# Tree layer: leaf rows fetched by index and summed late, with the last sums inside the attention behind it

## The reference, cut to what matters

```python
def _L0_ffn_ref(oldx, W_in, b_in, W_out):     # x: 2048 tokens of 256
    logits = x @ W_in.T + b_in                # 2048 x (8 * 255)
    decisions = (logits > 0).astype(jnp.int32).reshape(B, PAR, N_NODES)
    acts = jax.nn.silu(logits).reshape(B, PAR, N_NODES)
    current = jnp.zeros((B, PAR), dtype=jnp.int32)
    dmap = jax.nn.one_hot(current, N_NODES, dtype=acts.dtype)
    for d in range(DEPTH):                    # DEPTH = 7
        ...                                   # follow the decision one level down
        dmap = dmap + jax.nn.one_hot(current, N_NODES, dtype=acts.dtype)
    masked = acts * jax.lax.stop_gradient(dmap)
    out = masked.reshape(B, WIDTH) @ W_out.T
```

## Time and profile before

| | |
|---|---|
| median of 3 runs | 1630.63 us (1630.32 to 1631.8) |
| profiled execution | 1630.92 us, span 1629.2 us |
| PE busy | 1438.7 us, 88% |
| DVE busy | 1072.1 us, 66% |
| ACT busy | 755.6 us, 46% |
| POOL busy | 116.5 us, 7% |
| mean granted clock | 0.953 |

### The profile page before, as it was taken

How to read it: one execution, slowest core, us unless ns; L and a number is a source line. 1 busy time by engine, 2 the same in 40 slices (tenths; PEclk the granted TensorE clock), 3 DMA queues, 4 the chain that set the end, 5 groups by cost and what they waited for, 6 DMA issues and landing times.

```text
span 1629.2 us, 26350 instructions
## 1 busy us (share of the span) xinstructions
PE 1438.7 (88%) x9842; PEld 1074.1 (66%) x9849; DVE 1072.1 (66%) x2358; ACT 755.6 (46%) x1264; POOL 116.5 (7%) x168
## 2 busy tenths in 40 slices
PE   7999999878897996799989999999988889999557
PEld 5666666557783443477786878787764677788446
DVE  4455575778877874687866465655458988886344
ACT  2211212257773666376672222222224877788323
POOL 1000000000000000111000000000010011001323
PEclk9999999989998997899998999999998999999779
DMA  9462202320000000000008910000100000010166
GB/s 323 167 207 78 78 1 78 127 85 14 14 3 0 1 1 1 25 14 1 14 2 265 303 43 1 1 1 0 33 7 7 1 7 2 7 31 24 41 186 180
DMA packets 60285, 96.62 MB, mean 59 GB/s; under 512 B 11091, under 2 KB 48972, under 8 KB 59982
## 3 DMA queue, kind: packets, MB, share of 16 engines
q1 hardware_dynamic: 57742, 78.50, 15.0%
q10 hardware_dynamic: 544, 12.16, 2.2%
q0 software_dynamic: 1872, 4.27, 0.7%
HBM read 73.21 MB, written 37.30 MB: 68 GB/s over the span
## 4 chain that ended last, share of the span: by engine, by line
PE 50%; issue 18%; DVE 15%; ACT 6%; DVEq 4%; DMA 2%; SPq 1%; POOL 1%; ACTq 1%; POOLq 1%
PE bank L1997 8%; PE bank L1998 8%; PE bank L1689 7%; PE bank L1667 7%; DVE MB L927 3%; PE bank L1794 3%; DVE plo L945 2%; PE bank L1845 2%; PE bank L1595 1%; PE bank L1765 1%; PE bank L1799 1%; PE bank L1798 1%; DMA jx<-copy_routed 1%; DVE raw L1211 1%; PE bank L1767 1%
## 5 line engine op out<-in xcount | busy, mean ns | idle before, releaser
L945 DVE TENSOR_TENSOR plo<-e,phi 120x512 f16<-120x512 f32 x256 | 179.1, 705 | 50.2 <-ACT phi L1419 46.5
L1413 ACT ACTIVATE e<-bank 120x512 f32<-120x512 f32 x256 | 150.6, 588 | 42.7 <-PE bank L1799 34.3
L927 DVE TENSOR_REDUCE MB<-bank 128x4 bf16<-128x480 f32 x256 | 155.9, 646 | 15.1 <-PE bank L1767 11.5
L1419 ACT ACTIVATE phi<-e 120x512 f16<-120x512 f32 x256 | 161.2, 630 | 8.8
L1344 ACT ACTIVATE act<-bank,bin 127x512 f32<-127x512 f32 x64 | 43.1, 687 | 167.2 <-DVE dec L757 163.2
L1667 PE MATMUL bank<-xT,winT 128*127 128x512 f32 (+1 forms) x256 | 114.6, 593 | 1.3 <-ACTq L1315 1.3
L1689 PE MATMUL bank<-woutT,msk 128*128 128x256 f32 (+1 forms) x512 | 115.1, 379 | 0.0
L676 DVE TENSOR_SCALAR high<-raw 128x512 int32<-128x512 int32 x96 | 41.0, 427 | 108.1 <-ACT raw L1548 60.9
L1689 PEld LDWEIGHTS bank<-woutT,msk 128*128 128x128 f32 (+1 forms) x512 | 96.8, 190 | 15.4
L556 POOL TENSOR_TENSOR veps<-mv,ceps 128x4 f32<-128x4 f32 x32 | 8.9, 278 | 1336.7 <-DVEq L647 1204.9
L1997 PE MATMUL bank<-hah,h1w 128*128 128x512 f32 x256 | 101.3, 396 | 3.6 <-DVE hal L679 3.6
(11 more groups left out here) (308 smaller groups left out, 3518.8 us busy)
## 6 DMA issues: line engine op xcount, KB each, us to landing
copy_routed<-zeros SPq DMA_DIRECT2D x1, 17028.0 KB
jw<-copy_experts SPq DMA_DIRECT2D x23, 385.0 KB, 3.3
seen<-in_h1T SPq DMA_DIRECT2D x8, 512.0 KB, 7.2
seen<-in_h2T SPq DMA_DIRECT2D x8, 512.0 KB, 4.9
h1w<-copy_h1T SPq DMA_DIRECT2D x1, 4096.0 KB, 16.7
h2w<-copy_h2T SPq DMA_DIRECT2D x1, 4096.0 KB, 14.3
ctxp<-in_ctxT SPq DMA_DIRECT2D x13, 240.0 KB, 3.0
jx<-copy_routed SPq DMA_DIRECT2D x23, 132.0 KB, 3.1
```

Source lines behind the costliest of these rows:

```text
L927: dve.tensor_reduce(MB[:, t, h0 // 8, SK + h0 % 8:SK + h0 % 8 + 4], b[:, 0:4 * SK].rearrange("p (h k) -> p h k", h=4), AX.X, ALU.max).then ...
L945: dve.tensor_tensor(plo[:, g % 3, :], e32[:, g % 3, :], phi[:, g % 3, :], ALU.subtract).then_inc(s.lo, 1)
L1413: act.activation(e32[:, g % 3, :], bank[2 + g % 3][0:SK, :], ACT.Exp).then_inc(s.exp, 1)
L1419: act.activation(phi[:, g % 3, :], e32[:, g % 3, :], ACT.Copy).then_inc(s.phi, 1)
```

## The change

The leaf part of the dense products is replaced. Of all four pairs, 32 steps (`STEPS`) are now counted through, and `tree_step(g)` on each engine says what it does in step g, for itself and for older steps:

- Layer 0's attention gets transposes of the leaf columns of `winT` on PE in its last two pairs and copies on ACT into `table`; ACT and SP write `leaves`, a table in HBM with, for each of 1024 leaves, its output row (256), its input row (256) and its bias: 2052 bytes. The 1 MB load of the leaves' `woutT` falls away.
- Only inner nodes are multiplied densely: half the logits, one silu, one mask, half the output products.
- From the count of the leaves ACT makes a one-hot `hot` (a Relu of 128x512, bf16), PE multiplies it with the leaf numbers (four products of one column), and DVE writes the row number `idx`.
- POOL gathers the rows: four indirect transfers of 128 rows for each step, into one of five buffers `rowsG`.
- Four steps behind, DVE takes the dot of each token's normalised row with its leaf's input row (`leaf_logits`, four instructions with a running sum), and ACT the silu (`leaf_values`, four of one column) and three scaled identity matrices `dgl`.
- Five steps behind, PE adds three of the four tiles (`turned_leaves`, identity matrix times rows, into the sums' banks) and DVE the fourth, straight to x (`add_leaves`).
- The sums of two pairs lie in different banks, and normalised rows in two buffers. A pair's residual follows in the sixth step of the next pair.
- `low_bits` is one OR of each slice into `seen_low`; the test for the low bits comes once, at the end. Slices are spread over the steps.
- The five weight copies are issued in steps 3, 9, 14, 19 and 24 instead of before the stage, and the first mask of L1X is loaded at the start.
- Steps 34 to 37 (the last dots, values and sums and the last residual) stand on PE, ACT and DVE behind the first four steps of L1X. L1X on PE waits for the last residual only before its first `values`, and DVE for the turned sums of step 27.

The core of the diff:

```diff
+STEPS, ROW, GB, LAG = PAIRS * TREES, 2 * D + 1, 5, 5
+SUMS = (4, 0)
+TURNED = (0, 1, 2)
...
+        def gather(g):
+            pool.wait_ge(Tf.row, g + 1)
+            if g >= GB:
+                pool.wait_ge(Tf.added, g - GB + 1)
+                pool.wait_ge(Tf.turned, g - GB + 1)
+            for t in range(TT):
+                pool.indirect_dma_start(rowsG[g % GB][:, t, 0:ROW], None, leaves[:],
+                                        bass.IndirectOffsetOnAxis(idx[:, g % TREES, t:t + 1], 0),
+                                        bounds_check=TREES * LEAVES - 1, oob_is_err=False).then_inc(landed[g % GB], 16)
...
         def low_bits(i, q):
-            dve.tensor_scalar(seen_low[:], seen[:, q, :].bitcast(I32), 0xFFF, None, ALU.bitwise_and)
-            dve.drain()
-            dve.tensor_reduce(lowmax[:, ds(i * SEEN + q, 1)], seen_low[:], AX.X, ALU.max)
+            dve.tensor_tensor(seen_low[:], seen_low[:], seen[:, q, :].bitcast(I32), ALU.bitwise_or)
...
+        def leaf_logits(g):
+            rows_in = (xln, xln_odd)[g // TREES % 2]
+            dve.wait_ge(landed[g % GB], got(g))
+            for t in range(TT):
+                if t == 2:
+                    dve.drain()
+                last = dve.scalar_tensor_tensor(out=dots[:, t % 2, :], in0=rows_in[:, t, :], scalar=1.0,
+                                                in1=rowsG[g % GB][:, t, D:2 * D], op0=ALU.mult, op1=ALU.mult,
+                                                accum_out=lv[:, g % GB, t:t + 1])
+            dve.drain().then_inc(Tf.dot, 1)
...
+            def tree_step(g):                          # DVE
+                i, p = g // TREES, g % TREES
+                if g < STEPS and (p or not i):
+                    decisions(g)
+                if 1 <= g <= STEPS:
+                    masked(g - 1)
+                if 4 <= g < STEPS + 4:
+                    leaf_logits(g - 4)
+                if g == 2 * TREES:
                     weight_scales()
+                if 1 <= g <= STEPS:
+                    leaf_numbers(g - 1)
+                if 5 <= g < STEPS + 5:
+                    add_leaves(g - 5)
+                if g < STEPS and not p and i:
+                    decisions(g)
+                if g >= TREES and g % TREES == LAG % TREES:
+                    tree_residual((g - LAG) // TREES - 1)
...
+        def hot_leaves(g):
+            act.wait_ge(Bf.cnt, g + 1)
+            if g >= 2:
+                act.wait_ge(Tf.idx, g - 1)
+            act.activation(hot[:, g % 2, :], bank[7][:, :], ACT.Relu, bias=onec[:, 0:1]).then_inc(Tf.hot, 1)
+
+        def leaf_values(g):
+            act.wait_ge(Tf.dot, g + 1)
+            if g >= 2:
+                act.wait_ge(Tf.turned, g - 1)
+            for t in range(TT):
+                last = act.activation(val[:, g % GB, t:t + 1], lv[:, g % GB, t:t + 1], ACT.Silu,
+                                      bias=rowsG[g % GB][:, t, 2 * D:ROW])
+            act.drain()
+            for n, t in enumerate(TURNED):
+                last = act.activation(dgl[:, g % 2, n, :], ident[:], ACT.Copy, scale=val[:, g % GB, t:t + 1])
+            last.then_inc(Tf.val, 1)
...
+            def tree_step(g):                          # PE
+                if g < STEPS and (p or not i):
+                    tree_logits(g)
+                if i and not p:
+                    pe.wait_ge(Bf.act, g)
+                    transpose_rows(i + (4 + 1), 2, (xln, xln_odd)[i % 2])
+                if 1 <= g <= STEPS:
+                    right_turns(g - 1)
+                if 2 <= g < STEPS + 2:
+                    inner_outputs(g - 2)
+                if 1 <= g <= STEPS:
+                    leaf_number(g - 1)
+                if 5 <= g < STEPS + 5:
+                    turned_leaves(g - 5)
...
+                if g < STEPS and not p and i:
+                    tree_logits(g)
...
+                if L is L1X and step + n < LAG - 1:
+                    tree_step(STEPS + 2 + step + n)
```

## The result

The changed kernel takes 1645.17 us (median of 4 runs, 1644.34 to 1652.58) where the kernel before takes 1631.22 (median of 4, one run more than above): ratio 1.0083, interval 1.0065 to 1.010. It is slower by 13.5 to 14 us, where 21 us faster had been forecast. The profiled execution took 1644.34 us, its span is 1642.6.

What follows compares the result with a forecast made beforehand. PE was taken to bound the tree stage. First maximum from 323.2 to 297.2, less 1.5 for the residual, saves 24.5; less 3.5 for clock and lining up, 21 us: 1610 us, range 1593 to 1636.

Steps and rivals of the forecast that it cites:

- rival D: Tree stage: cheaper dots (1.7 us) and no lining-up loss, intervals go to PE's 5.7 us, 1590 us; chance 0.07.
- C: Tree stage: Relu makes ACT reload tables, 1.28 us twice a step, time near 1670 us; chance 0.03.
- what hides the gathers: Tree stage: POOL's four gathers cost 5.1 us a step, under 6.3; rows have 15 us against 9.2 needed.
- landing takes 3.9: Tree stage: gathered rows land in 3.9 us, on top of 5.3 us.
- a cover of 6 us: Tree stage: dots read rows 15 us or more after their number, against 9.2 us for issuing and landing.
- also holds for the copies: Tree stage: the gathers' 6 us cover was said to hold for the weight copies on ACT's queue too.
- Now they are spread: Tree stage: the five weight copies, all in the first pair before (DMA share 0.66), are now spread.
- the rest of SP is unmoved: SP queue: the mask load is earlier, seen loads stay paced by DVE, everything else stays; no size given.
- PE's clock falls inside the stage: Tree stage: sign that the forecast is wrong; PE had been expected at clock 1.00, about 86% busy.
- (A): Tree stage: POOL sets the pace; break-even 1.75 us a transfer, 1634 us at 1.78, 1661 at 2.0; chance 0.20.
- (B): Tree stage and tail: DVE's dots cost 2.7 us instead of 2.1, time 1626 us; chance 0.15.
- DVE waits for rows: Tree stage: sign that the forecast is wrong, with POOL busy throughout; no DVE wait on landing was expected.

Runs made afterwards that it cites:

- e13: Changed kernel with all three edits of e4, plus eight more drains at the head of VectorE's program: 1610.57 us, ratio 0.9862.
- e4: Changed kernel with drain replaced by a semaphore, weight copies and their loads moved later, second mask and context loads issued earlier: 1618.55 us, ratio 0.9917.
- e9: The kernel of e4 run again on a third chip: 1617.38 us, ratio 0.9913.
- e14: Changed kernel with all three edits of e4, plus twenty more drains at the head of VectorE's program: 1614.67 us, ratio 0.9887.
- e1: Changed kernel with only POOL's drain ahead of the tree stage's `rstd` replaced by a semaphore: 1629.07 us, ratio 0.9979.
- e2: Changed kernel with only the five weight copies moved into the first-layer attention and the loads reading them behind its loop: 1628.01 us, ratio 0.9971.
- e3: Changed kernel with only SP's order changed, second mask and context loads issued ahead of the 7 MB of weight loads: 1640.03 us, ratio 1.0049.
- e6: Control: kernel before, with its five copies issued in L1X's loop and the loads that read them behind it: 1635.25 us, ratio 1.0015.
- e17: Changed kernel with nothing but eight more drains at the head of VectorE's program: 1644.68 us, ratio 1.0070.
- e8: Kernel of e4 with the tree stage's end (steps 34 to 37) in one piece ahead of L1X's first units: 1642.71 us, ratio 1.0065.
- e16: Kernel of e4 with the tree stage's end in one piece, run beside the shifted kernels: 1625.02 us, ratio 0.9945.
- e5: Changed kernel with drain replaced by a semaphore and copies with their loads moved later, mask and context loads left in place: 1639.02 us, ratio 1.0038.

## Why the prediction was wrong

**Right, with small errors.** The first decision is at 75.93 (76.0 forecast). Undisturbed intervals are 5.56 to 5.63 us (5.7), the turn of a pair 10.19 (10.5), a pair's first interval 1.72 (1.7). From first to last decision e13 takes 188.0 us (189.9): the first pair 2.5 us more than its share, as leaving out the first four steps' leaves saved 3.5 and not 6, the others 4.4 less. The tail from last decision to first maximum is 31.8 (31.3). Dots follow one another at 0.35 us, not 0.47, with a read of the sum of 0.08 within: rival D's price. It bought nothing in plain intervals, which PE's round sets, and about 0.5 us in those with an OR beside the rows or the residual (6.2 to 6.3 for 6.8). Relu brought no table load (C falls). DVE's two waits for the queries are 0.9 and 1.2, not 2 each. With the waits gone the sum comes out up to the first maximum: in e13 the last decision is at 265.1 for 265.9 and the first maximum at 296.8 for 297.2. That e13's 1610.57 us hits the forecast's 1610 is in part luck: the same edits without a moved pause give 1618.55 and 1617.38 (e4, e9), with another shift 1614.67 (e14). The engines' work was priced rightly, and the error was in what no engine's busy time shows.

**Wrong, first: the step "what hides the gathers".** It lists POOL's four issues a step and the landing, and leaves out POOL's own queue: `rstd_of` follows the gathers of each pair's first step, and its drain waits until they have landed. It is the question "what is queued behind", not asked for a drain. POOL stood 25.2 us in four pieces, DVE 9.5 in all for `rstd`. e1 puts the price at 16 us of time, and at 19 between first and last decision: nearly the whole loss of the stage.

**Wrong, second: "landing takes 3.9", with "a cover of 6 us", which "also holds for the copies".** The 3.9 came from the earlier trace rows, and it was no quiet stretch: the kernel before in the stretch of those scatters, then e2 in the tree stage, length, PE, PEld, DVE, ACT, POOL busy, clock, DMA share, GB/s.

```profile
1570.00:1629.00 59.00, 48.02 (x303) 39.37 (x301) 30.94 (x109) 21.46 (x64) 22.64 (x23) 0.99 0.67 203
```

```profile
76.00:290.00 214.00, 187.99 (x783) 123.82 (x781) 167.01 (x457) 99.27 (x282) 147.57 (x134) 0.93 0.65 202
```

At the same load the same 3.9 came out. What failed is "also holds for the copies". The gathers alone are 33.6 MB, and with five copies spread among them the share is 0.75 to 0.90 between 131 and 251 us, where the kernel before has 0.14 (136 to 256 us). The cover was 6 us on top of 3.9, so it ends at a landing of 9.9 us: 17 of e3's 116 gathers took longer, up to 18.1. The longest wait for rows, 7.2 us at 178 while `copy_h1T` was under way, held the leaf numbers and through them PE, 6.0 us. With the drain gone little of this is left (e1), so the two steps failed together: the copies made the gathers late, and the drain made lateness dear. e2 takes the copies away, and e6 shows that the kernel before has no use for this. "Now they are spread" was said as a comfort; it laid them beside gathers all through the stage.

**Wrong, third: "the rest of SP is unmoved".** Its instructions are; their time is not. SP issues the weight loads once the last residual is through, and this residual now comes behind the first units' maxima. The use of the second mask, first in the kernel before, then in the kernel after:

```profile
337.29 0.73 DVE L878 TENSOR_SCALAR MB<-m 128x480 bf16<-128x480 int32 x2 [0.24 <-issue]
```

```profile
342.82 0.73 DVE L1000 TENSOR_SCALAR MB<-m 128x480 bf16<-128x480 int32 x2 [10.49 <-DMA m<-in_mask]
```

In the kernel before the mask is issued at 316.9 in the wake of the loads and lands 17.2 us later, 3 us ahead of its use. In the kernel after it is issued at 325.4, 8.5 us later, and lands 17.3 us later, while the attention around it wants it at 332.3, 5 us earlier. So the mask was always slow, and the change used up its margin from both sides. e3 puts the price at 7.4 us in the trace and 5 in the time.

**Not in the forecast: the last stage.** 3.9 us, which go with DVE's pause and the clock behind it (e13, e14, e17). In the trace of the kernel before no such pause stands in this stretch, so no view of it could have shown where one would fall. The sign "PE's clock falls inside the stage" came true as well (0.91 to 0.97), but it is no explanation of the loss: e4 and e13 have 0.95 and 0.97 there (77 to 265 us).

**The rivals.** (A), POOL's pace, is not what happened: a gather takes 1.13 us on average with 0.30 behind, 1.43 for a break-even of 1.75, and POOL is idle between. The change ended on A's side of the range all the same, by another mechanism of the same queue. Beside some operations of DVE gathers do stretch, at most from 1.00 to 2.14 us (timeline of the kernel after):

```profile
212.06 1.31 DVE L775 TENSOR_SCALAR stage_w<-stage_w,stage_ws 128x2048 f32<-128x2048 f32 x1
212.65 2.14 POOL L627 DMA_INDIRECT rows<-copy_leaves,idx  x1 [0.30 <-issue]
```

The Trainium skill, SBUF - State Buffer, SBUF: two separate sides, gives 620 ns alone and some 3100 beside a DVE copy for a DMA issued from GpSimd. The trace agrees in direction; the stretch here is 2.14 us for 1.00, in 12 of 128 gathers more than 1.5. (B) is refuted by the 0.35. The chance for "slower", 0.16, was too low, since it held only A and C; no rival had a transfer that lands late, though the prediction gave "DVE waits for rows" as its own sign of failure.

**The two halves of the change.** Together they are worth 13.5 to 16 us over the kernel before once their waits are gone (e4, e9), and 22 with the pause elsewhere (e13). The end between the attention's first units makes 4 to 6 of that (e8, e16). The version with all three edits and the shift is the fastest here: 1610.57 us, 1.4% below the kernel before.

**What stays open.** Why e5 and e8 were 20 us slower on one chip, whose runs of the kernel before are as fast as elsewhere (1632.99). In their traces DVE and ACT have waits of up to 4 and 8 us in the tree stage put down to a "remote" releaser, which no other trace has; together 17 us on DVE in e5. They stand at the same places in both (4.2 us ahead of a decision and 7.7 ahead of a silu at 237 us). They are not only the tree stage's: one of 3.0 us is in the last stage, which takes 56.3 us in both for 49.9 elsewhere. Of the kernels that ran there only those with gathers show them, but that the gathers cause them is not shown. What DVE's pause itself is was not tested: the runs show that it is bound to the place in the program and 0.27 to 0.44 us long. And e1's and e2's prices are not apart: they overlap by about 7 us. A kernel with the drain and the order on SP mended and the copies left in the stage wasn't run; by e1 and e3 it should come close to e4.

## What to carry to other kernels

When transfers go to an engine's queue, go through everything else on that queue and ask of each drain and wait what it now waits for; a drain behind gathers costs their landing. Take a landing time from a stretch as loaded as the one it is used in, and add up everything that will run there: 3.9 us held at a DMA share of 0.65, and no longer with the copies on top. An instruction that isn't moved still moves in time when what releases it does, and with it all that is queued behind; ask how much margin its result has, and from which side the change eats it.

## What the runs showed of the hardware

- A drain on GpSimd between two of its 0.2 to 1.2 us operations took 8.96 us with gathers outstanding; with a semaphore in its place the gap was 0.08. In eight cases with every landing in the trace the next operation started 0.31 or 1.44 to 1.45 us behind the last landing (e2, e3).
- A gather of 128 rows of 2052 B takes GpSimd 1.00 us and 0.30 to the next one, up to 2.1 to 2.3 beside VectorE; it lands after 3.9 us (median; 3.4 to 9.1) at a mean of some 200 GB/s (e2). With copies among them, between 131 and 192 us, it lands after 8.0 (3.5 to 18.1; e3).
- A product with a running sum, both inputs f32 of 256 columns in SBUF, has a pitch of 0.35 us; the read of the sum is 0.08 within it.
- Pauses of 0.27 to 0.44 us on VectorE, with no wait, move when instructions are put in ahead of them; with one of them moved, the granted clock in the 5 us behind its old place was 1.00 and not 0.66.
- One and the same kernel with 128 gathers took 1639.0 us on one chip and 1618.4 on another, where the kernel without them took 1633.0 and 1633.1.
